# A GNN layer with routed experts: the self-loop term moved from TensorE and GpSimd to VectorE

## The reference, cut to what matters

```
deg  = maximum((adj != 0).sum(-1), 1)
dinv = rsqrt(deg)
# graph layer, on h = layernorm(x)
a_norm = dinv * (adj + I) * dinv          # dinv multiplies each row of (adj + I) twice: 1/deg
pooled = a_norm @ h + h
x = x + relu(pooled @ W + b)
# then: x = x + (top-1 expert of layernorm(x)) + shared_ffn(layernorm(x))
```

## Time and profile before

| | us |
|---|---|
| median of three runs | 507.82 |
| the profiled execution | 510.69 |
| its span, first to last instruction | 509.1 |
| PE (TensorE) busy | 457.6 |
| DVE (VectorE) busy | 270.9 |
| ACT (ScalarE) busy | 197.2 |
| POOL (GpSimd) busy | 322.3 |

### The profile page before, as it was taken

How to read it: one execution, slowest core, us unless ns; L and a number is a source line. 1 busy time by engine, 2 the same in 40 slices (tenths; PEclk the granted TensorE clock), 3 DMA queues, 4 the chain that set the end, 5 groups by cost and what they waited for, 6 DMA issues and landing times.

```text
span 509.1 us, 8980 instructions
## 1 busy us (share of the span) xinstructions
PE 457.6 (90%) x2652; PEld 391.9 (77%) x2653; DVE 270.9 (53%) x558; ACT 197.2 (39%) x434; POOL 322.3 (63%) x299
## 2 busy tenths in 40 slices
PE   5899977999999989899687999699979999999992
PEld 5778756897789878798565888588868888888871
DVE  4997799917692569767451343233423333343330
ACT  3555721663456454745241333122322232232230
POOL 3889865487857786576065584857475848887111
PEclk9999989999999999999897999799989999999997
DMA  7574150503160251719869777787878787465000
GB/s 255 185 217 154 49 165 13 165 2 117 49 206 1 76 174 43 253 42 321 233 198 322 240 249 257 257 267 232 276 237 280 241 274 232 56 71 73 8 1 0
DMA packets 40876, 82.61 MB, mean 162 GB/s; under 512 B 4880, under 2 KB 16528, under 8 KB 38800
## 3 DMA queue, kind: packets, MB, share of 16 engines
q1 hardware_dynamic: 25792, 45.11, 28.8%
q0 software_dynamic: 7536, 29.39, 18.9%
q10 hardware_dynamic: 7520, 7.77, 4.9%
HBM read 74.74 MB, written 8.41 MB: 163 GB/s over the span
## 4 chain that ended last, share of the span: by engine, by line
PE 41%; DVE 15%; DMA 11%; POOL 10%; issue 6%; ACT 2%; SPq 1%; POOLq 0%; DVEq 0%; ACTq 0%
PE bank L1208 16%; DMA eraw<-in_experts 7%; POOL ering L413 6%; PE bank L1233 6%; PE bank L1126 5%; DVE count L729 4%; PE bank L1145 4%; DMA ering<-in_experts 4%; POOL a_lo L366 3%; DVE rows L705 3%; PE bank L1234 3%; PE bank L1219 2%; PE bank L1147 2%; PE bank L1040 1%; DVE resid L795 1%
## 5 line engine op out<-in xcount | busy, mean ns | idle before, releaser
L413 POOL TENSOR_TENSOR ering<-eraw,ering 128x512 fp32r<-128x512 f32 x84 | 105.7, 1286 | 75.1 <-DMA ering<-in_experts 37.4
L1208 PE MATMUL bank<-ering,xsT_hi 128*128 x368 | 125.8, 414 | 11.6 <-POOL ering L413 7.5
L366 POOL TENSOR_TENSOR a_lo<-araw,a_hi 128x512 fp32r<-128x512 f32 x64 | 93.6, 1480 | 30.3 <-ACT a_hi L500 30.1
L1040 PE MATMUL bank<-zz,a_hi 128*128 128x512 f32 (+1 forms) x256 | 93.3, 404 | 7.0 <-POOL a_lo L366 6.9
L1208 PEld LDWEIGHTS bank<-ering,xsT_hi 128*128 128x128 f32 x368 | 72.1, 196 | 29.4 <-issue 12.7
L959 DVE SCALAR_TENSOR_TENSOR hid<-bank,xs,sil 128x512 f32<-128x512 f32 x46 | 34.5, 751 | 111.0 <-ACT sil L625 109.0
L1208 PE MATMUL bank<-ering,xsT_lo 128*128 x184 | 75.0, 408 | 0.0
L625 ACT ACTIVATE sil<-bank 128x512 f32<-128x512 f32 x46 | 27.5, 599 | 119.7 <-PE bank L1208 119.7
L1042 PE MATMUL bank<-zz,a_lo 128*128 128x256 f32 (+1 forms) x256 | 72.2, 282 | 0.0
L1233 PE MATMUL bank<-ering,hidT_hi 128*128 x184 | 67.8, 408 | 1.2 <-DVE hidT_lo L967 1.2
L1040 PEld LDWEIGHTS bank<-zz,a_hi 128*128 128x128 f32 x256 | 48.8, 191 | 20.0 <-issue 8.4
(11 more groups left out here) (151 smaller groups left out, 809.4 us busy)
## 6 DMA issues: line engine op xcount, KB each, us to landing
eraw<-in_experts SPq DMA_DIRECT2D x96, 256.0 KB, 3.3
araw<-in_adj_t SPq DMA_DIRECT2D x32, 512.0 KB, 5.0
ering<-in_experts POOLq DMA_DIRECT2D x8, 1536.0 KB, 7.4
ering<-in_experts POOLq DMA_DIRECT2D x8, 1024.0 KB, 7.1
ering<-in_experts POOLq DMA_DIRECT2D x8, 512.0 KB, 5.9
xs<-sorted_x ACTq DMA_DIRECT2D x23, 129.0 KB
resid<-in_x SPq DMA_DIRECT2D x4, 512.0 KB, 8.8
sw_raw<-in_sw_t ACTq DMA_DIRECT2D x2, 1024.0 KB, 7.0
```

Of the source, the lines that this page charges most:

```text
L366: pool.tensor_tensor(a_lo[:, u % AR, :], araw[:, u // CJ, u % CJ, :], a_hi[:, u % AR, :].bitcast(F32), ALU.subtract).then_inc(adj_lo_ok, 1)
L413: pool.tensor_tensor(ering[:, slot, 1, c * ECW:(c + 1) * ECW], eraw[:, c % ER, :], ering[:, slot, 0, c * ECW:(c + 1) * ECW].bitcast(F32), ...
L1040: pe.matmul(acc(it)[:, :], a_hi[:, s, it * P:(it + 1) * P], zt, start=first, stop=False)
L1208: ins = pe.matmul(bank[2 * w + h][:, :], a[:, k, :], ering[:, bass.ds(slot, 1), part, at:at + BANK].rearrange("p a n -> p (a n)"), start=n ...
```

## The change

The self-loop no longer passes through TensorE. `agg_end` and `ident_r` are gone (the last `agg_part` of a quarter closes the accumulation), the sixteen additions of the bias on GpSimd are gone, and VectorE makes z * (1/deg + 1) + bias in `finish_gnn`, by one small operation and four of 128x256 per quarter. `copy_sums` waits for the quarter's sixteenth `agg_part`. Two chunks of quarter 1 are counted between `inverse_degree(0)` and `finish_gnn(0)`; two fewer are counted after it.

```
@@ places
-    ident_r = place("ident_r", [P, P], F32R)
+    self_part = place("self_part", [P, QT], F32)
@@ GpSimd, first_lows
-                pool.wait_ge(bias_loaded, 16)
                 for t in range(NT):
                     adj_low(t % (RAW * CJ), t)
-                    pool.wait_ge(z_copied, t + 1)
-                    pool.tensor_tensor(norm[:, t, :], norm[:, t, :], bias[:], ALU.add).then_inc(bias_added, 1)
@@ ScalarE
-            act.activation(ident_r[:], ident[:], ACT.Copy).then_inc(split_hi, 1)
@@ ScalarE, copy_sums
-                act.wait_ge(agg_sum, q + 1)
+                act.wait_ge(agg_tile, (q + 1) * NT)
@@ VectorE, finish_gnn
+                dve.wait_ge(dinv_ok, q + 1)
+                dve.wait_ge(z_copied, (q + 1) * QT)
+                chained(dve.tensor_scalar(self_part[:], dinv2[:], 1.0, None, ALU.add))
+                settle()
+                if q == 0:
+                    dve.wait_ge(bias_loaded, 16)
+                for it, t in enumerate(group(q)):
+                    chained(dve.scalar_tensor_tensor(norm[:, t, :], norm[:, t, :], self_part[:, it:it + 1],
+                                                     bias[:], ALU.mult, ALU.add))
                 dve.wait_ge(agg_free, (q + 1) * QT)
-                dve.wait_ge(dinv_ok, q + 1)
-                dve.wait_ge(bias_added, (q + 1) * QT)
+                settle()
@@ VectorE, order
             sum_halves(0)
             inverse_degree(0)
+            count_chunks(1, 0, 2)
             finish_gnn(0)
             for q in range(1, NQ):
-                count_chunks(q, 0, RAW)
+                count_chunks(q, 2 if q == 1 else 0, RAW)
@@ TensorE
-                                    start=False, stop=False)
+                                    start=False, stop=last)
-            def agg_end(q):
-                for it in range(QT):
-                    ins = pe.matmul(acc(it)[:, :], ident_r[:], zz[:, q * QT + it, :, :].rearrange("p h d -> p (h d)"),
-                                    start=False, stop=True)
-                ins.then_inc(agg_sum, 1)
```

More of the change, by code:

```diff
@@ L215, in gnn_moe @@
         z_copied = sem("z_copied")
-        bias_added = sem("bias_added")
         adj_hi_ok = sem("adj_hi_ok")
@@ L220, in gnn_moe @@
         agg_tile = sem("agg_tile")
-        agg_sum = sem("agg_sum")
         deg_ps = sem("deg_ps")
@@ L504, in _ @@
             stds(0)
-            act.wait_ge(consts, 1)
-            act.activation(ident_r[:], ident[:], ACT.Copy).then_inc(split_hi, 1)
             act.wait_ge(w_loaded, 16)
@@ L735, in _ @@
             dve.wait_ge(w_loaded, 16)
-            dve.wait_ge(split_hi, 2)
+            dve.wait_ge(split_hi, 1)
             dve.tensor_tensor(w_lo[:], w_raw[:], w_hi[:].bitcast(F32), ALU.subtract).then_inc(split_lo, 1)
@@ L757, in split_shared @@
             def split_shared():
-                dve.wait_ge(split_hi, 3)
+                dve.wait_ge(split_hi, 2)
                 dve.tensor_tensor(gate_r[:, :, E:2 * E], gate_raw[:], gate_r[:, :, 0:E].bitcast(F32),
                                   ALU.subtract).then_inc(split_lo, 1)
-                dve.wait_ge(split_hi, 5)
+                dve.wait_ge(split_hi, 4)
                 dve.tensor_tensor(sw1_lo[:], sw1_raw[:], sw1_hi[:].bitcast(F32), ALU.subtract
@@ L1026, in z_tile, with agg_part @@
                 ins.then_inc(z_ps, 1)
-            def agg_part(j, s, n, first=False):
+            def agg_part(j, s, n, first=False, last=False):
                 pe.wait_ge(adj_lo_ok, n + 1)
@@ L1074, in _ @@
                 pe.wait_ge(z_ok, t + 1)
-                agg_part(t, t % AR, t)
+                agg_part(t, t % AR, t, last=t == NT - 1)
             pe.wait_ge(z_copied, NT)
-            agg_end(0)
             degrees(0)
@@ L1087, in agg_quarter @@
                 for j in range(TURN, NT):
-                    agg_part(j, j % AR, q * NT + j)
-                agg_end(q)
+                    agg_part(j, j % AR, q * NT + j, last=j == NT - 1)
             def xf_transposes(q):
```

## The result

The changed kernel has a median of 515.2 us (513.77 to 516.8, four runs) against 507.35 for before (four runs): a ratio of 1.0156, interval 1.0133 to 1.018, so 7.9 us slower where 3.6 were forecast. Its profiled execution took 514.64 us, with a span of 512.8; the one of before lay 3.3 us above its own median, which is why the two profiles differ by less than the medians. So the comparison goes by the same instructions on the clock of the span, up to the one that lets the padding and the experts' loads begin (`fill_row`, the table of rows to pad). Each number is of one execution. Six profiled kernels of this document share the changed code up to `sum_halves(0)`, which begins at 53.14 to 53.83 in them; in three with the code of before it begins at 55.05 to 55.20. So the gain there is 1.3 to 2.0 us, 1.5 in the mean, and the changed kernel's profile shows the least of it.

A forecast was written before the change was run, and what follows sets the result against it. VectorE was taken to bound the first stage and quarter 1. First stage -2.1, quarter 1 +2.9, quarter 3 +1.9 and its clock +0.9 summed to +3.6 us on the median 507.82: 511.4 us, range 505.5 to 514.5.

The forecast's parts named there:

- First stage, -2.1: Up to `sum_halves(0)`: 1.8 us from dropped bias additions plus 0.33 from dropped identity matmuls, 2.1 us earlier (0.3 to 3.7).
- Quarter 1 on VectorE, +2.9: Up to the second normalization: 1.8 us of added work and eleven `a_lo` collisions (11.6 against 10.5), +2.9 us (-1.5 to +4.5).
- But TensorE was not the bound.: Quarter 1: early counts remove ScalarE's 6.55 us DMA wait and TensorE's 3.27, but VectorE bounds there; no gain counted.
- Ends of quarters 1 and 2, 0: Added operations fit VectorE's 4.19 us idle before `add_shared`; low-part collisions fit TensorE's slack: 0, at most 0.5 us each.
- Quarter 3, +1.9: Uncovered finish on VectorE: 0.2 + 1.6 us added and one or two collisions, less savings: 1.9 us (1.6 to 2.7).
- The clock in quarter 3, +0.9 at even odds: TensorE's wait grows to about 3.5 us; a fall to 1.2 GHz costs 1.7 us, about even odds, so 0.9.
- rival 1: Faster: the DMA stall removed by early counts was worth more than the collisions, quarter 1 -1.5: 504.9 us; chance 0.18.
- Rival 3: Slower by more: first stage -1.0, quarter 1 +4.0, quarter 3 +2.5, clock falls +1.7: +7.2, 515.0 us; chance 0.10.

The follow-up runs named there:

- late counts: The changed kernel with the early counts of two chunks of quarter 1 undone, the rest of the change kept: 511.49 us, ratio 1.0106 against before.
- one residual operation: The changed kernel with the four relu-and-residual operations of a finish made one of 128x1024: 513.12 us, ratio 1.0101 against before.

## Why the prediction was wrong

The direction was right, the size was not: 3.6 us against 7.9. The step that failed is TensorE's clock. The sum had nothing for it in quarter 1, without a reason, and 0.9 us in quarter 3; the runs showed 0.88 and 2.00 us, and gave both back when idle transposes filled the waits. That is 2.0 of the 3.0 us by which the front of the kernel exceeds the sum (6.6 against 3.6). The rest is in the first stage (0.8, of which 0.3 is this execution's) and in quarter 3's work on VectorE (0.65), less 0.4 in quarter 1. By the steps of the sum:

1. *First stage, -2.1.* Measured -1.26 here, -1.5 in the mean of six profiles. Of the three places where TensorE could gain, the first gave nothing (its wait was 1.74 us before and 1.68 after, and ended at 17.77 and 17.98). The two groups of four tiles behind it got shorter by 0.5 us each (10.65 and 10.67 us before, 10.15 and 10.12 after), half of the 1.1 that was the most they could give. Left out of the kernel before, the bias additions gave 1.7 in all. The identity matmuls were priced at 0.33 and gave 0.25.
2. *Quarter 1 on VectorE, +2.9.* Measured +2.46. The collisions came as counted: eleven `a_lo`, none beside the statistics. Eight short operations met one each, where nine were expected. By the prediction's own length without collisions (15.5 + 1.8 = 17.3 us) the 28.5 us from 55.52 to 84.06 hold 11.2 us of excess, 1.02 us for each `a_lo` and not 1.05. What the prediction said of the cause is too narrow: it put the collisions down to operations with two inputs in SBUF, but its own example L705 reads one tensor there (beside two columns of factors) and went from 0.41 to 1.42 us.
3. *"But TensorE was not the bound."* This is where the sum first failed. TensorE was not the bound, but its wait for the rows grew to 10.07 us, and I did not price the clock after it, though the earlier trace rows had the price and the step for quarter 3 used it. At 1.2 GHz the transposes and tiles 12 to 15 took longer, VectorE waited for both in turn, and 0.88 us was lost. The idle transposes gave it back to the hundredth.
4. *Ends of quarters 1 and 2, 0.* Measured 0.04.
5. *Quarter 3, +1.9.* Measured +2.55. The self-loop part took 3.37 us (203.59 to 206.96), with two collisions that made operations of 0.48 us into 0.95 and 1.39; what followed saved 0.8. This lies within the step's own bounds (1.6 to 2.7).
6. *The clock in quarter 3, +0.9 at even odds.* Measured +2.00. Averaging a loss that either happens or not was the weak point: a wait of 3.5 us was forecast where the trace had one of 3.27 with the fall; the wait became 4.38. The price of a fall, 1.7 us, was near the measured one by luck. It was worked out for some 3.4 us at the low clock; behind the 4.38 us wait the clock read 0.50 from 216 to 222. Where it was low for about half as long, with late counts (213 to 216) and with one residual operation, the stretch to `fill_row` lost 0.8 and 1.0 us. With the fall taken for the likeliest in quarter 3, and the 0.9 us that quarter 1 lost by it, known only now, the sum would have been +5.3 (-2.1 + 2.9 + 0.9 + 1.9 + 1.7).
7. The front of the kernel makes 6.6 us, the medians 7.9. For the 1.2 us between no run tells what they are. Behind `fill_row` one profile differs from another by more than that: 275.7 to 282.2 us in eleven.

On rival 1: the early counts removed the DMA stall as it said, and the time got longer, not shorter. Rival 3 had the clock falling, and a time (515.0) near the measured one, but for other reasons: its first stage and quarter 1 were worse than measured, and the clock in quarter 1 was not in it.

## What to carry to other kernels

When work moves to an engine that bounds a stage, price the other engines' new waits too: a wait of some microseconds on TensorE is free only as long as its clock survives it, and filling it with idle transposes tells at once whether it does. A stall that is taken away on an engine with slack may buy nothing, as here, and can line up work that collides. When an experiment leaves out part of the computation, compare instructions upstream of the first place where data steer the time, not totals.

## What the runs showed of the hardware that was not expected

What VectorE and GpSimd lose by keeping each other out is counted by the GpSimd operations: merging four VectorE operations of 128x256 (3.63 us beside two `a_lo`) into one of 128x1024 (1.23 us) shortened the stretch by 0.65 us only, since two of the counts behind it went from 1.23 to 2.08 us, with twelve `a_lo` in both. GpSimd pays too: an `a_lo` of 1.27 us took 2.27 beside such a count.

Between the first stage and `fill_row` TensorE kept its full clock after waits of 1.56 and 2.75 us and lost it after 3.21, 3.27 (before, quarter 1), 3.30, 4.38, 5.38, 6.80, 7.86, 9.00 and 10.07 us; idle transposes of the identity kept it at full speed through waits that had cost it. The length of the last wait alone does not decide it, though. In the experts' stage of the kernel before the clock reads 0.50 behind a wait of 2.66 us, shorter than the 2.75 us that kept it:

```profile
378.97 0.79 PE L1208 MATMUL bank<-ering,xsT_hi 128*128 x1 [2.66 <-POOL ering L413]
...
379.00:380.00 1.00, 1.00 (x3) 0.50 0.29 40
```
